# The last row of y in two halves of 256 rows: two layer norms around products with a 4096 x 4096 matrix

## The reference, cut to what matters

```python
scale = sum(d_list * filt * d_list, axis=0)                 # 4096
x1 = layernorm(x + adj @ (scale[:, None] * (adj @ (x @ weight))) + bias)
deg_in = sum(adj, axis=1); deg_out = sum(adj.T, axis=1)     # where > 0, else 1
y = (adj / deg_in) @ x1 @ W_in                              # rows of adj
z2 = (adj.T / deg_out) @ x1 @ W_out                         # columns of adj
out = layernorm(x1 + y + z2)                                # over the 128 features, eps 1e-5
```

## Time and profile before

| | |
|---|---|
| median of 3 runs | 735.02 us (734.94 to 735.05) |
| the profiled execution | 734.96 us, span 733.1 us |
| PE busy | 726.4 us, 99% |
| DVE busy | 598.0 us, 82% |
| ScalarE busy | 522.6 us, 71% |
| HBM read | 219.58 MB, mean of all traffic 302 GB/s |

### The profile page before, as it was taken

One profiled execution on the slowest core, in us unless ns is written; L12 is line 12 of the kernel. 1 busy time (PEld: TensorE's weight loads), 2 busy tenths in 40 slices (PEclk: granted clock), 3 DMA queues, 4 the chain that ended last, 5 costly groups with the idle time before them and its releaser, 6 DMA issues.

```text
span 733.1 us, 9244 instructions
## 1 busy us (share of the span) xinstructions
PE 726.4 (99%) x3293; PEld 600.8 (82%) x3293; DVE 598.0 (82%) x754; ACT 522.6 (71%) x1336; POOL 18.6 (3%) x15
## 2 busy tenths in 40 slices
PE   9999999999999999999999999999999999999997
PEld 5888888888888888888888888888888888888885
DVE  6898997756363888998786778997898999899996
ACT  6888888737354639467374547998989898777673
POOL 1112400000000000000000000000000000000000
PEclk9999999999999999999999999999999999999999
DMA  9999999456443677666646469999989999999991
GB/s 371 426 425 423 425 427 387 173 179 229 173 173 118 226 266 307 232 268 247 230 175 266 157 213 390 381 386 389 367 325 391 385 368 379 379 362 352 357 367 34
DMA packets 36109, 222.27 MB, mean 303 GB/s; under 512 B 3680, under 2 KB 8544, under 8 KB 9568
## 3 DMA queue, kind: packets, MB, share of 16 engines
q1 hardware_dynamic: 35792, 221.56, 78.4%
q10 hardware_dynamic: 272, 0.13, 0.1%
HBM read 219.58 MB, written 2.10 MB: 302 GB/s over the span
## 4 chain that ended last, share of the span: by engine, by line
PE 99%; DVE 0%; ACT 0%; issue 0%; DVEq 0%; ACTq 0%
PE accA L716 13%; PE accA L721 13%; PE accB L716 13%; PE accB L721 13%; PE accA L726 13%; PE accB L726 13%; PE accC L721 6%; PE accC L716 6%; PE accC L726 6%; PE nat L775 3%; PE accB L821 1%; PE nat L782 0%; DVE stats L685 0%; ACT rows L428 0%; DVE accC L590 0%
## 5 line engine op out<-in xcount | busy, mean ns | idle before, releaser
L469 DVE TENSOR_TENSOR lo<-raw,hi 128x2048 fp32r<-128x2048 f32 (+2 forms) x249 | 476.1, 1937 | 86.0 <-ACT hi L325 74.8
L325 ACT ACTIVATE hi<-raw 128x512 fp32r<-128x512 f32 x512 | 315.4, 622 | 68.8 <-DMA raw<-in_adjT_b 42.4
L716 PE MATMUL accA<-hi,x_hi 128*128 128x512 f32 x416 | 163.3, 393 | 0.1
L721 PE MATMUL accA<-hi,x_lo 128*128 128x512 f32 x416 | 161.9, 389 | 0.0
L726 PE MATMUL accA<-lo,x_hi 128*128 128x512 f32 x416 | 116.4, 389 | 0.0
L716 PE MATMUL accB<-hi,v_hi 128*128 128x512 f32 x256 | 100.0, 391 | 0.0
L721 PE MATMUL accB<-hi,v_lo 128*128 128x512 f32 x256 | 99.6, 389 | 0.0
L330 ACT ACTIVATE hi<-raw 128x512 fp32r<-128x512 f32 x158 | 86.8, 621 | 17.2 <-DMA raw<-in_adjT_b 17.1
L325 ACT ACTIVATION_READ_ACCUMULATOR hi<-raw 128x1 f32 x512 | 97.6, 191 | 0.0
L716 PEld LDWEIGHTS accA<-hi,x_hi 128*128 128x128 f32 x416 | 78.2, 188 | 17.2 <-issue 1.2
L726 PEld LDWEIGHTS accA<-lo,x_hi 128*128 128x128 f32 x416 | 78.1, 188 | 16.3
(11 more groups left out here) (102 smaller groups left out, 502.1 us busy)
## 6 DMA issues: line engine op xcount, KB each, us to landing
raw<-in_adjT_b SPq DMA_DIRECT2D x143, 1024.0 KB, 5.8
raw<-in_adj_b SPq DMA_DIRECT2D x64, 1024.0 KB, 5.1
rows<-in_x_b SPq DMA_DIRECT2D x8, 256.0 KB, 9.6
out<-rows SPq DMA_DIRECT2D x7, 256.0 KB, 6.1
out<-rows SPq DMA_DIRECT2D x1, 128.0 KB, 1.8
out<-rows ACTq DMA_DIRECT2D x1, 128.0 KB, 2.1
coef<-in_coef_t SPq DMA_DIRECT2D x1, 96.0 KB, 9.0
w<-in_W SPq DMA_DIRECT2D x1, 64.0 KB, 9.0
```

The costliest lines, as they stand in the source:

```text
L325: nc.scalar.activation(hi[slot][:, t], raw[slot][:, t], ACT.Copy, accum_out=to[:, TPB * K + t, C:C + 1]).then_inc(s_hi, 1)
L469: nc.vector.tensor_tensor(lo[slot][:, at], raw[slot][:, at], hi[slot][:, at], ALU.subtract).then_inc(s_lo, 1)
L716: nc.tensor.matmul(acc, r_hi[:, TPB * K + t], h[:, t], start=(first and t == 0), stop=False)
L721: nc.tensor.matmul(acc, r_lo[:, TPB * K + t], h[:, t], start=False, stop=False)
```

## The change

Row 7 of y is kept in two accumulators, each of 256 rows (columns of the tile): accA[:, 1, 0:256] and the upper half of the nat bank that is free by then. Its first five chunks are done by `by_halves`, with both halves in turn for each operand. The last three (`SPLIT`) are done for the first half throughout, and then for the second. So the first half is complete three half chunks ahead of the second; ScalarE copies it, and PE multiplies its tiles 0 and 1 by w_in behind the first half chunk of the second half. DVE does statistics, root and scaling per half. The w_out product of the last z2 is done for all four tiles at the old early place, and all four are added to the banks there. The lo of the last chunk is made in two parts, by columns. The inverse root is written as h / (h * h + var), h being the square root from ScalarE, in three dependent steps in place of four (rstd is the same Newton step). At the end one tile is scaled and stored by DVE and SP, one by ScalarE and its queue; tiles 0 and 1 are stored before.

```diff
@@ -127,6 +127,8 @@
+    SPLIT = list(range(N4 - 3, N4))
...
@@ -251,15 +254,18 @@
+        s_half = sem("first_half_of_last_row_done")
...
+        FREE = NAT_Y[NB - 1] - 2
+        last_acc = [accA[:, 1, 0:2 * P], nat[:, FREE % 2, 2 * P:4 * P]]
@@ -310,7 +316,9 @@
             sp.wait_ge(s_fin, 1)
             store(sp, NB - 1, range(0, 2))
-            sp.wait_ge(s_st, 16 * (NB + 1))
+            sp.wait_ge(s_fin, 2)
+            store(sp, NB - 1, range(2, 3))
+            sp.wait_ge(s_st, 16 * (NB + 2))
@@ -404,31 +412,35 @@
+                if n == N4 - 1:
+
+                    act.wait_ge(s_half, 1)
+                    act.wait_ge(s_n, NAT_Y[NB - 1])
+                    nc.scalar.activation(turned[:, 1, 0:2 * P], accA[:, 1, 0:2 * P], ACT.Copy).then_inc(s_lh, 1)
...
-            for at in (slice(0, P), slice(P, 2 * P), slice(2 * P, 4 * P)):
-                nc.scalar.activation(turned[:, 1, at], accA[:, 1, at], ACT.Copy).then_inc(s_lh, 1)
             k = 2 * NB - 1
             act.wait_ge(s_var, k + 1)
-            nc.scalar.activation(std[:, k % 2], last_var[:], ACT.Sqrt).then_inc(s_std, 1)
+            nc.scalar.activation(std[:, k % 2, 0:2], last_var[:, 0:2], ACT.Sqrt).then_inc(s_std, 1)
+            act.wait_ge(s_rel, rank[N4 - 1])
+            for t in (2, 3):
+                to = slice(P * t, P * t + P)
+                nc.scalar.activation(turned[:, 1, to], nat[:, FREE % 2, to], ACT.Copy).then_inc(s_lh, 1)
+            act.wait_ge(s_var, k + 2)
+            nc.scalar.activation(std[:, k % 2, 2:4], last_var[:, 2:4], ACT.Sqrt).then_inc(s_std, 1)
+
             act.wait_ge(s_neg, 1)
...
+            t = TPB - 1
+            row = TPB * (NB - 1) + t
+            nc.scalar.activation(rows[:, row], last_bank[t][:, P * t:P * t + P], ACT.Identity,
+                                 bias=shift[:, k % 2, t:t + 1]).then_inc(s_cen, 1)
             act.wait_ge(s_cen, 1)
...
+            act.wait_ge(s_rs, NB + 1)
+            nc.scalar.activation(rows[:, row], rows[:, row], ACT.Copy,
+                                 scale=rstd[:, k % 2, t:t + 1]).then_inc(s_out, 1)
             act.wait_ge(s_out, NB)
-            store(nc.scalar, NB - 1, range(2, 4))
+            store(nc.scalar, NB - 1, range(3, 4))
@@ -459,6 +471,12 @@
+                if n == N4 - 1:
+                    dve.wait_ge(s_hi, hi_at[n][TPB - 1])
+                    for at in (slice(0, 2 * P), slice(2 * P, 4 * P)):
+                        nc.vector.tensor_tensor(lo[slot][:, :, at], raw[slot][:, :, at], hi[slot][:, :, at],
+                                                ALU.subtract).then_inc(s_lo, 1)
+                    return
@@ -595,7 +613,7 @@
-                for t in range(2 if J == NB - 1 else TPB):
+                for t in range(TPB):
@@ -676,33 +694,38 @@
...
+            for half in range(2):
+                tiles = range(2 * half, 2 * half + 2)
+                at = slice(2 * half, 2 * half + 2)
+
+                for t in tiles:
+                    dve.wait_ge(s_n, NAT_Y[r] + t + 1)
+                    last = nc.vector.bn_stats(stats[:, t], last_bank[t][:, P * t:P * t + P])
+                then(last)
+                for t in tiles:
+                    last = nc.vector.bn_aggr(mv[:, k % 2, t], stats[:, t])
+                then(last)
+                nc.vector.scalar_tensor_tensor(last_var[:, at], mv[:, k % 2, at, 1], 0.25, last_eps[:, at],
+                                               ALU.mult, ALU.add).then_inc(s_var, 1)
...
+                dve.wait_ge(s_var, k + 1 + half)
+                dve.wait_ge(s_std, k + 1 + half)
+                h, q = std[:, k % 2], newt
+                for t in tiles:
+                    last = nc.vector.scalar_tensor_tensor(q[:, t:t + 1], h[:, t:t + 1], h[:, t:t + 1],
+                                                          last_var[:, t:t + 1], ALU.mult, ALU.add)
+                then(last)
+                then(nc.vector.reciprocal(q[:, at], q[:, at]))
+                nc.vector.tensor_tensor(rstd[:, k % 2, at], q[:, at], h[:, at], ALU.mult).then_inc(s_rs, 1)
+                dve.wait_ge(s_rs, NB + half)
+                for t in tiles[:2 - half]:
+                    last = nc.vector.tensor_scalar(rows[:, TPB * r + t], last_bank[t][:, P * t:P * t + P],
+                                                   mv[:, k % 2, t, 0:1], rstd[:, k % 2, t:t + 1],
+                                                   ALU.subtract, ALU.mult)
+                last.then_inc(s_fin, 1)
@@ -871,7 +894,25 @@
-            for n in range(N2, N4):
+            def by_halves(J, n):
+
+                cols = (slice(0, 2 * P), slice(2 * P, 4 * P))
+                pe.wait_ge(s_hi, hi_at[n][0])
+                for t in range(TPB):
+                    for half in range(2):
+                        nc.tensor.matmul(last_acc[half], x_hi[:, TPB * J + t], hi[slot_of[n]][:, t, cols[half]],
+                                         start=(J == 0 and t == 0), stop=False)
+                    for half in range(2):
+                        nc.tensor.matmul(last_acc[half], x_lo[:, TPB * J + t], hi[slot_of[n]][:, t, cols[half]],
+                                         start=False, stop=False)
+                pe.wait_ge(s_lo, lo_at[n][0])
+                for t in range(TPB):
+                    for half in range(2):
+                        mm = nc.tensor.matmul(last_acc[half], x_hi[:, TPB * J + t], lo[slot_of[n]][:, t, cols[half]],
+                                              start=False, stop=False)
+                mm.then_inc(s_rel, 1)
+
+            for n in range(N2, SPLIT[0]):
@@ -887,7 +928,12 @@
-                    product(accA[:, I % 2], x_hi, x_lo, J, n, J == 0, J == I).then_inc(s_rel, 1)
+                    if I == NB - 1:
+                        if J == 0:
+                            pe.wait_ge(s_nat, FREE + 1 - NB)
+                        by_halves(J, n)
+                    else:
+                        product(accA[:, I % 2], x_hi, x_lo, J, n, J == 0, J == I).then_inc(s_rel, 1)
@@ -895,27 +941,45 @@
...
+                    by_rows(NAT_H[J], turned[:, NAT_H[J] % 2] if J < NB - 1 else last_z2_turned, w_out)
...
+            def w_in_last(t):
+
+                to = slice(P * t, P * t + P)
+                nc.tensor.matmul(last_bank[t][:, to], turned[:, 1, to], w_in[:], start=False, stop=True).then_inc(s_n, 1)
+
+            for half, at in enumerate((slice(0, 2 * P), slice(2 * P, 4 * P))):
+                for n in SPLIT:
+                    J, I = chunks[n]
+                    acc, h, l = last_acc[half], hi[slot_of[n]], lo[slot_of[n]]
+                    if half == 0:
+                        pe.wait_ge(s_hi, hi_at[n][0])
+                    for t in range(TPB):
+                        nc.tensor.matmul(acc, x_hi[:, TPB * J + t], h[:, t, at], start=False, stop=False)
+                        nc.tensor.matmul(acc, x_lo[:, TPB * J + t], h[:, t, at], start=False, stop=False)
+                    if half == 0:
+                        pe.wait_ge(s_lo, lo_at[n][0])
+                    elif n == N4 - 1:
+                        pe.wait_ge(s_lo, lo_at[n][0] + 1)
+                    for t in range(TPB):
+                        mm = nc.tensor.matmul(acc, x_hi[:, TPB * J + t], l[:, t, at], start=False,
+                                              stop=(n == N4 - 1 and t == TPB - 1))
+                    if half == 1:
+                        mm.then_inc(s_rel, 1)
+                    elif n == N4 - 1:
+                        mm.then_inc(s_half, 1)
+                    if half == 1 and n == SPLIT[0]:
+                        pe.wait_ge(s_nat, NAT_H[NB - 1] + 1 - NB)
+                        pe.wait_ge(s_lh, 1)
+                        w_in_last(0)
+                        w_in_last(1)
             for t in (2, 3):
...
+                pe.wait_ge(s_lh, t)
+                w_in_last(t)
```

More of the change, by code:

```diff
@@ L152, in graph_kernel @@
         hi_count, lo_count = hi_at[n][-1], lo_at[n][-1]
+    assert max(w_in_at) < SPLIT[0] and max(w_out_at) < SPLIT[0] and lo_at[N4 - 1][0] == lo_count
     NAT_O = NB
@@ L238, in graph_kernel @@
         s_std = sem("deviation_ready")
-        s_lh = sem("last_half_turned")
-        s_cen = sem("last_tiles_centred")
+        s_lh = sem("parts_of_last_row_turned")
+        s_cen = sem("last_tile_centred")
         s_out = sem("out_ready")
@@ L253, in graph_kernel @@
         s_fin = sem("last_tiles_ready")
-        s_hl = sem("last_z2_added")
-        s_neg = sem("last_means_negated")
+        s_neg = sem("last_mean_negated")
         s_dve = sem("dve_step")
         s_rel = sem("chunks_released")
+        s_half = sem("first_half_of_last_row_done")
         s_z1 = sem("z_done")
@@ L678, in _ @@
             dve.wait_ge(s_out, k - NB - 1)
[L680 to L705, removed]
+            for half in range(2):
[11 more added lines that the diff above has]
+                if half == 1:
+                    nc.vector.tensor_scalar(shift[:, k % 2, 3:4], mv[:, k % 2, 3:4, 0], -1.0, None,
```

(8 more changed lines are left out.)

11 lines of the change are left out of this document (removed).

## The result

The changed kernel takes 735.72 us, median of 22 runs, against 734.89 of the kernel before in its 22: 0.83 us more, or 0.11%. The comparison over all runs gives a ratio of 1.0017, with a 95% interval of 1.0011 to 1.0022. It lies above that of the medians, as the means differ by 0.16%: seven of the 22 runs of the changed kernel lie 0.6 to 3.2 us above their median, and none of the kernel before lies more than 0.4 above its own. Why is not shown. The difference is about the 0.2% that I had called no change, but it is clear of zero, and on the other side of zero from the forecast of 734.4. It lies on rival 1, the fixed price of an instruction (735.7). The profiled executions say the same: 735.72 after, 734.96 before.

What follows compares the result with a forecast made beforehand. TensorE, busy 99% of the span, was taken as the bound, with a 6.94 us tail behind it. 734.96 + 0.90 (stream) + 0.00 (matmul size) - 1.53 (tail) = 734.33, with 0.06 734.4 us; range 733.7 to 736.0.

Steps and rivals of the forecast that it cites:

- rival 1: Last row's matmuls: a fixed price per instruction makes 256 columns cost 0.120 us, +1.3 us, 735.7 in all; chance 0.22.
- The size of the matmuls: Last row: 192 matmuls of 256 columns for 96 of 512, taken as proportional, 0.1133 us each, 0 us.
- The bound from above: Last row: all 0.0134 us of surplus at 512 columns is fixed per instruction, so 256 cost 0.120 us, +1.3 us.
- The root: Tail: four steps of 0.88 us become three and a hand-over, 0.72 us, so 0.16 us less.
- z2 in the stream: PE's stream: two more tiles of the last z2 at the early place, 4 x 0.113 = 0.45 us more.
- w_in: Product for tiles 0 and 1 moves from tail into PE's stream: +0.45 us, its wait for ScalarE's copy hidden, 0.7 to spare.
- The last stores: End of the tail: stores of 64 KB each and not 128, halving DMA busy time, 0.43 us less.
- DVE's side: DVE in the last row: the first part of the last lo is ready 0.4 us before PE wants it; all hidden.
- Rival 2: Last row: the weight load becomes the pace, 0.124 us a matmul or over, up to 748.7 us; chance 0.09.
- Rival 3: Overlap lost: PE waits for lo's first part or ScalarE copies the second half late, 0.5 to 1 us, 735.1; chance 0.10.
- rival 4: A better stream: 0.110 us a matmul and the full gain of the stores, 733.7 us; chance 0.09.
- The signs: Profile marks: wrong if the 256-column pitch is over 0.12 or second-half statistics start over 0.9 us after the last product.

Runs made afterwards that it cites:

- e3: The kernel before plus unread extra matmuls of 512 to 64 columns behind its last one; executed once, only for pitches: fp32r 120 ns at 256 columns.
- e2: The kernel before with the last row's 96 matmuls of 512 columns made 191, 190 of them of 256, in one bank: 736.05 us against 734.91.
- e1: The changed kernel with the last row's first five chunks 512 columns wide again, their sum saved and added by VectorE: 734.97 us.
- e4: The changed kernel with the root in four steps again, two columns at a time: 735.65 us.
- e5: The kernel before with only the last z2's small product done for all four tiles at the early place: 735.42 us against 734.98.
- e7: The changed kernel with SyncE storing tiles 0 to 2 together at the end, 256 KB left there and not 128: 736.12 us.

## Why the prediction was wrong

*The step that failed* is the choice inside "The size of the matmuls": "I take 0.1133, thus 0 us, since the nearest row, with the same stream and the same kind of load, gives 0.111 and not 0.120." The pitch is 0.120, and the term is +1.28 us. The row that I called nearest, eight fp32 instructions 0.111 apart, showed the floor of the pitch, by all appearance the weight load's: e3 gives the same pitch at 64 columns. It could not say what the matmul itself costs when the floor is not the limit. Its duration did not tell the length of its stream either, as I had assumed: in e3 it is nearly the same for 64 columns as for 128. The bound from above, 0.0134 us of surplus at 512 columns taken as fixed, was the true value at 256, and e3, e2 and e1 show it in three ways. With +1.28 the sum gives 734.33 + 1.28 = 735.61.

*The root* saves 0.04 and not 0.16: the pair of one-column products takes 0.38 to the next step (730.58 to 730.96), not 0.24, a figure for which the prediction had no row. By e4 only 0.01 of the 0.04 comes from the new form. That is the other 0.12: 735.73, against the profiled 735.72.

*Right, by their steps.* z2 in the stream +0.45 and nothing for L910 (e5 shows 0.39 in its trace and 0.44 in its median for both together). w_in +0.45, its copy hidden. Statistics of two tiles end at 729.77, 1.41 behind the last product, as forecast; aggregates, scaling (0.40) and the root's start follow. The last stores: from the end of the last scaling to the span's end it was 733.1 - 730.57 = 2.53 us and is 733.9 - 731.82 = 2.08, 0.45 less where 0.43 was forecast, and e7 shows what it hangs on. DVE's side: no wait of PE at lo. The tail was forecast at 5.4 us and is 5.54.

*The rivals.* Rival 1 came, by its mechanism. That its 735.7 is met to 0.02 is in part luck: the root's 0.12, which it did not have, is offset by the 0.06 between median and profiled execution, which did not return, and by roundings. Rival 2 did not come: loads overlap, and the floor of 0.111 lies below 0.120. But it was nearer than I wrote, since at 192 columns it would decide. Rival 3 and rival 4 did not come. My 0.22 for rival 1 was too low; the range held the time, the sign was wrong.

*The signs.* A step of 2.88 us a chunk was to speak for rival 1, and it is there. But what was to prove the prediction wrong, a pitch over 0.12, was set at the very value that rival 1 gives, and the statistics start 0.88 us behind the last product where over 0.9 was asked; neither sign fires, though the term was wrong. A sign has to lie between the forecast and its nearest rival, here at 0.117.

*What stays open.* The source of the 13.3 ns of an fp32r matmul was not looked for; the runs show only that it depends on the type, is the same at 256, 320 and 512 columns (in the products), and not a matter of the bank; at 448 it is nearer 16. No version that beats the kernel before was found: e1 is its equal. Its halves still pay 0.48 us for 72 narrow matmuls and 0.90 for what moved forward, against 1.4 of tail.

## What to carry to other kernels

When PE is the bound, a split of its matmuls is not free, as e2 shows: count the instructions and price each by the surplus of the wide one over its columns, here 13.3 ns for fp32r, and never under the floor, here 111 ns. Before a row is used as the nearest one, ask what sets it; a row that stands on the floor bounds its own matmul from above and says nothing of a wider one. An overlap that needs work to move into the full engine's stream should be balanced against the idle time it had at its old place, and the split kept to the chunks that the overlap needs.

## What the hardware showed

Three numbers that the prediction did not have. With a granted clock of 1.00, an fp32r matmul costs its columns at 2.4 GHz plus 13.3 ns at 256 and 512 columns, bf16 plus 2.5. With a weight load for each, fp32 and fp32r matmuls start 111 to 112 ns apart in e3 at 192, 128 and 64 columns alike. And a one-column scalar_tensor_tensor on DVE with a per-partition scalar (L718) takes 0.22 us on the mean of four, against 0.16 for the four-column one without such a scalar (L690 before). One column alone is not what makes it slow: the one-column L711 takes 0.15.
